# Scaling the memory part of a gated attention on ScalarE instead of VectorE, one head sooner, with another bank order for the last head

## The reference, cut to what matters

```python
q, k, v = x @ Wq.T, x @ Wk.T, x @ Wv.T
qh = q.reshape(b, s, N_QUERY, N_HEAD, D_HEAD)        # 4, 8, 16: 32 heads
scores = jnp.einsum('bsqhd,bthd->bqhst', qh, kh) * scale
probs = jax.nn.softmax(scores, axis=-1)
a_dot = jnp.einsum('bqhst,bthd->bsqhd', probs, vh)
sigma_q = jax.nn.elu(q.reshape(b, s, N_QUERY, D_KV))  # D_KV = 128
a_mem = sigma_q @ memory / (sigma_q @ memory_norm)
w = jax.nn.sigmoid(memory_weight)
out = a_dot * (1.0 - w) + a_mem * w
```

## Time and profile before

| what | us |
|---|---|
| median of 3 runs | 5107.09 |
| lowest and highest | 5098.03, 5112.65 |
| the profiled execution's own time | 5093.37 |
| its span, first to last instruction | 5091.6 |
| PE busy | 4591.6 (90%) |
| DVE busy | 3620.3 (71%) |
| ACT busy | 2409.6 (47%) |
| POOL busy | 716.3 (14%) |

### The profile page before, as it was taken

How to read it: one execution, slowest core, us unless ns; L and a number is a source line. 1 busy time by engine, 2 the same in 40 slices (tenths; PEclk the granted TensorE clock), 3 DMA queues, 4 the chain that set the end, 5 groups by cost and what they waited for, 6 DMA issues and landing times.

```text
span 5091.6 us, 144724 instructions
## 1 busy us (share of the span) xinstructions
PE 4591.6 (90%) x63104; PEld 3229.5 (63%) x63104; DVE 3620.3 (71%) x7890; ACT 2409.6 (47%) x4592; POOL 716.3 (14%) x909
## 2 busy tenths in 40 slices
PE   5799999999999998499999999999999999999998
PEld 4677777777777776346546645655654664665564
DVE  3667766666767666387787678678778767867866
ACT  3234333333333343164564565466456456546645
POOL 0000000000000000112211211221221121122121
PEclk9899999999999998699999999999999999999999
DMA  2222222222222222100000000000000000000000
GB/s 61 48 66 69 65 65 67 61 62 61 62 61 65 64 68 61 64 1 18 1 18 18 18 1 18 18 2 18 18 2 18 18 13 6 18 18 1 18 9 10
DMA packets 352134, 171.76 MB, mean 34 GB/s; under 512 B 300016, under 2 KB 300784, under 8 KB 350736
## 3 DMA queue, kind: packets, MB, share of 16 engines
q1 hardware_dynamic: 342528, 145.20, 10.7%
q10 hardware_dynamic: 8976, 17.30, 1.2%
HBM read 93.74 MB, written 67.63 MB: 32 GB/s over the span
## 4 chain that ended last, share of the span: by engine, by line
PE 43%; DVE 10%; ACT 3%; issue 1%; POOL 1%; DMA 1%; SPq 0%; DVEq 0%; ACTq 0%; POOLq 0%
PE row_psum L1687 9%; PE row_psum L1661 9%; PE row_psum L40 5%; DVE smax L1938 5%; PE row_psum L42 5%; PE row_psum L41 5%; PE row_psum L1675 4%; PE row_psum L1729 1%; ACT xr_hi L1310 1%; PE row_psum L1713 1%; DVE probs L1918 1%; PE row_psum L1451 1%; DVE stats L1772 1%; POOL rstd L1253 1%; PE row_psum L1633 1%
## 5 line engine op out<-in xcount | busy, mean ns | idle before, releaser
L1938 DVE TENSOR_REDUCE smax<-row_psum 128x1 f32<-128x512 f32 x2048 | 1269.3, 681 | 90.9 <-PE row_psum L1661 90.4
L1386 ACT ACTIVATE probs<-row_psum 128x512 f32<-128x512 f32 x2048 | 1096.6, 602 | 378.1 <-PE row_psum L1675 358.5
L1661 PE MATMUL row_psum<-k_stack,q_stack 64*128 64x512 f32 (+1 forms) x2048 | 738.3, 437 | 50.6 <-DVE smax L1938 24.4
L1675 PE MATMUL row_psum<-q_stack,k_stack 64*128 64x512 f32 (+1 forms) x2048 | 761.6, 447 | 17.4 <-DMA q_stack<-shift 4.4
L1661 PEld LDWEIGHTS row_psum<-k_stack,q_stack 64*128 64x128 f32 (+1 forms) x2048 | 350.5, 186 | 504.1 <-DVE smax L1938 374.0
L1687 PE MATMUL row_psum<-probs,v_aug 128*32 128x512 f32 x4096 | 539.5, 604 | 2.3 <-ACT av_sb L1402 0.8
L1675 PEld LDWEIGHTS row_psum<-q_stack,k_stack 64*128 64x128 f32 (+1 forms) x2048 | 340.9, 185 | 211.7 <-ACT probs L1386 152.3
L868 DVE TENSOR_TENSOR lane_t<-lane_t,lane_p 128x30 f32<-128x30 f32 (+14 forms) x960 | 318.3, 332 | 33.0
L40 PE MATMUL span_bank<-x_hi,w_hi 128*128 128x256 f32 x1024 | 303.1, 296 | 32.5 <-DVE x_lo L841 32.5
L865 DVE TENSOR_TENSOR lane_p<-lane_t 128x30 f32<-128x30 f32 (+14 forms) x960 | 315.6, 329 | 23.5
L40 PE MATMUL row_psum<-wf_hi,xr_hi 128*128 128x320 f32 (+1 forms) x1024 | 327.1, 319 | 0.5 <-DVE xr_lo L1806 0.3
(11 more groups left out here) (209 smaller groups left out, 9867.4 us busy)
## 6 DMA issues: line engine op xcount, KB each, us to landing
x_sp<-in_x ACTq DMA_DIRECT2D x33, 512.0 KB, 4.0
tri_dram<-tri SPq DMA_DIRECT2D x256, 64.0 KB, 2.0
lane_t<-tri_dram SPq DMA_DIRECT2D x32, 512.0 KB, 4.7
inv_dram<-lane_t SPq DMA_DIRECT2D x32, 512.0 KB, 2.6
inv_b<-inv_dram SPq DMA_DIRECT2D x256, 64.0 KB, 2.3
x_res<-in_x SPq DMA_DIRECT2D x32, 512.0 KB, 3.9
x<-x_res SPq DMA_DIRECT2D x32, 512.0 KB, 3.7
xs<-x SPq DMA_DIRECT2D x16, 1024.0 KB, 5.6
```

Of the source, the lines that this page charges most:

```text
L1386: act.activation(probs[:, h % PROBS, tt, :], ps[:, m % STACK_BANKS, :], ACT.Exp, scale=float(DH) ** -0.5).then_inc(exp_ready, 1)
L1661: pe.matmul(ps[:, bank, :], q_stack[rows, qt, P * st:P * st + P], k_stack[rows, kv, :], start=True, stop=True).then_inc(max_mm, 1)
L1675: pe.matmul(ps[:, m % STACK_BANKS, :], k_stack[rows, kv, P * tt:P * tt + P], q_stack[rows, qt, :], start=True, stop=True).then_inc(score_m ...
L1938: dve.tensor_reduce(smax[:, g, st:st + 1], ps[:, bank_of("max", NT * g + st), :], AX.X, ALU.max).then_inc(max_ready, 1)
```

## The change

`MEM_LAG` goes from 5 to 4, so the memory steps are at heads 4 to 7 and bank 7 enters the ring at step 8. DVE only takes the reciprocals and weights them; ACT, behind its two exponentials (or q copies) and the shift copy of the step's second half, scales four products of 128 columns by one column each of `mem_rc` and signals `amem_ready`. For the four maxima of head 31 the ring passes bank 7 over.

```diff
-MEM_LAG = 5
+MEM_LAG = 4
...
-                        put("max", NT * g + st)
+                        put("max", NT * g + st, next(n for n in order if g < NH - 1 or n != RING_LAST))
...
+                def memory(t):
+                    act.wait_ge(mem_rc_ready, at(b, NT, t + 1))
+                    for n in range(NQ):
+                        c0 = (DKV + 1) * (n % 2)
+                        last = act.activation(a_mem[:, t, DKV * n:DKV * n + DKV], ps[:, 6 + n // 2, c0:c0 + DKV], ACT.Copy,
+                                              scale=mem_rc[:, t, n:n + 1])
+                    last.then_inc(amem_ready, 1)
...
+                        if j == 1 and 0 <= g - MEM_LAG < NT:
+                            memory(g - MEM_LAG)
...
                     mark(dve.reciprocal(rc, pv[:, :, :, DKV]))
                     dve.wait_ge(dve_own, own[0])
-                    mark(dve.tensor_scalar(rc, rc, mem_w[:, 0:1], None, ALU.mult))
-                    dve.wait_ge(dve_own, own[0])
-                    for c in range(2):
-                        last = dve.tensor_tensor(a_mem[:, t, 2 * DKV * c:2 * DKV * c + 2 * DKV].rearrange("p (n e) -> p n e", n=2),
-                                                 pv[:, c, :, 0:DKV],
-                                                 rc[:, c, :].rearrange("p (n o) -> p n o", o=1).to_broadcast([P, 2, DKV]), ALU.mult)
-                    last.then_inc(amem_ready, 1)
+                    dve.tensor_scalar(rc, rc, mem_w[:, 0:1], None, ALU.mult).then_inc(mem_rc_ready, 1)
```

More of the change, by code:

```diff
@@ L1135, in token_layers @@
         ksel_mm = sem("ksel_mm"); keven_ready = sem("keven_ready"); kodd_ready = sem("kodd_ready"); qsel_mm = sem("qsel_mm"); qstack_ready = sem("qstack_ready")
-        mem_mm = sem("mem_mm"); amem_ready = sem("amem_ready"); amem_added = sem("amem_added")
+        mem_mm = sem("mem_mm"); mem_rc_ready = sem("mem_rc_ready"); amem_ready = sem("amem_ready"); amem_added = sem("amem_added")
         max_mm = sem("max_mm"); max_ready = sem("max_ready"); maxT_mm = sem("maxT_mm"); shift_ready = sem("shift_ready"); shift_in = sem("shift_in")
```

## The result

| | us | against the kernel before, run beside it |
|---|---|---|
| changed kernel, median of 7 runs | 5124.7 (5114.0 to 5131.7) | 1.0056 [1.0037, 1.0074] |
| kernel before, median of 7 runs | 5098.0 (5089.9 to 5112.7) | |
| changed kernel, profiled execution | span 5124.5 | before: 5091.6 |

The change makes the kernel 0.56% slower, 28.5 us by the ratio. The forecast was +13.0 us, or 5120.1. That time is only 4.6 us off, and this is luck in good part: the kernel before now has a median 9 us lower (5098.0 of 7 runs for 5107.1 of 3). Of the difference that came, the forecast had half, and its +13 us, a ratio of 1.0025, lie outside the interval. It had given the case within 0.3% a chance of 0.48 and the case slower by more, which came, 0.39.

The account below looks back on a forecast made before the run. The loop over banks 6 and 7, level with DVE's own work, was taken to bound the memory stretch. Its 27.4 us loss less 14.4 gained at the last head gave +13.0, 5120.1 us against the 5107.1 median; range 5095 to 5140.

Parts of the forecast that it names:

- the loop level with DVE: Heads 5 to 8: loop of reciprocals, scaling, PE's memory matmuls and maxima paces equally with DVE's own work, 0.08 us apart.
- ACT's group: Four scaling copies of 128x128 on ACT per memory step: 1.18 us, bounds 0.83 and 1.48.
- The forecast for the loop: From DVE's max(g,2), head g's tile 2 reduction, through ACT's scaling to PE's memory matmuls: 2.30 us, before 1.88.
- PE's parts: From PE's memory matmuls to DVE's next max(g,2): 1.89 us at head 5, 2.36 at head 6, 1.64 at head 7.
- The part behind the last tile: Head 8: max(8,0) takes bank 7 and waits for the last scaling; PE's part from there to DVE is 0.54 us.
- The start: Memory matmuls of tile 0 now precede q pick 10 on PE, making max(4,2) 0.35 us late.
- The memory stretch: Up to max(8,3), head 8's last reduction: 17.84 us instead of 16.13, so 1.71 us more a batch, 27.4 in all.
- From max(8,3) on, DVE's stream is unbroken in both: After head 8's last reduction DVE runs without breaks before and after the change, with no further cost counted.
- The last head: Head 31: PE's 1.60 us wait for the last maxima goes; 0.85 us gained in 15 batches, 1.6 once, 14.4 in all.
- gives all 1.6: Rival at the last head: the whole 1.6 us wait is gained each batch, total +1.8 us, 5109; chance 0.08.
- only moves: Rival at the last head: the wait moves wholly to the normalised rows' transposes, total +27.4 us, 5134.5; chance 0.08.
- the dearer ACT group: Rival: ACT's scaling group costs over 1.22 us; 1.27 gives +18.4 us (5125.5), 1.48 gives +32.2 (5139); chance 0.31.

Follow-up runs that it names:

- experiment 4: Changed kernel with two ACT copies of 128x256 per group instead of four of 128x128, half the heads using a neighbour's divisor: 5089.0 us, ratio 1.0001 to the kernel before.
- experiment 8: experiment 6 with PE's memory matmuls and DVE's reciprocals moved behind each head's fourth maximum, ACT scaling: 5041.8 us, ratio 0.9934 to the kernel before.
- experiment 9: The order of experiment 8 with the scaling on DVE instead of ACT: 5060.8 us, ratio 0.9968 to the kernel before.
- Experiment 5: Changed kernel with eight extra matmuls on PE ahead of the wait of max(8,0), their results overwritten: 5111.4 us, ratio 1.0042 to the kernel before.
- experiment 6: Changed kernel with bank 7 joining the ring at step 9 instead of 8: 5080.0 us, ratio 1.0011 to the kernel before.
- experiments 7: The kernel of experiment 2 with bank 7 joining the ring at step 9, scaling on DVE: 5091.4 us, ratio 1.0032 to the kernel before.
- experiment 2: Kernel before with memory steps at heads 4 to 7 and the last head's new bank order, scaling still on DVE: 5104.9 us, ratio 1.0020.
- experiment 3: Changed kernel with MEM_LAG 5 again, so ACT scales but memory steps stay at heads 5 to 8: 5128.4 us, ratio 1.0070 to the kernel before.
- experiment 1: Kernel before with only the new bank order for the four maxima of head 31: 5072.5 us, ratio 0.9963.

## Why the prediction was right, and where it fell short

- **The kernel's bound, the loop level with DVE: right.** Experiments 4, 8 and 9 show it from three sides: the shorter group shortens every turn, and with a short loop DVE's own work sets 3.54 us a head, as it did at heads 7 and 8 before.
- **ACT's group, 1.18 us: right,** 1.14 measured. (The 775 ns that the prediction sets beside the Trainium skill's figures, which by two pointer operands give an estimate of 798 ns, are 3% under them and not 2%; nothing hangs on it.) The forecast for the loop, 2.30 us from max(g,2) to PE's matmuls, came out at 2.27 (2393.34 to 2395.61, 2397.51 to 2399.78), and PE's parts 1.89, 2.36, 1.64 at 1.90, 2.37, 1.63. The part behind the last tile, 0.54, is 0.50 with the clock at full speed (2592.93 to 2593.43 in batch 2) and 0.80 in batch 1.
- **The start, 0.35 us late: 0.47.** max(4,2) before began at 2388.46, as the next reduction in a group of ten stands 0.60 behind the last, not 0.618; dividing a group's time by its count took the tail of the last one in. After, it is 2393.34 - 2389.28 = 4.06 us behind the same place instead of 3.59.
- **The memory stretch, +1.71 us a batch: +1.60 in a clean batch** (0.47 + 17.38 against 16.25, up to max(8,3)). Of the forecast idle times, 1.4, 1.8, 1.1 and 1.3, the trace has 1.34, 1.81, 1.06 and 1.23 (1.53 where the clock has fallen).
- **"From max(8,3) on, DVE's stream is unbroken in both": wrong after the change.** Before, 18 reductions run on to 2415.7, and 0.37 us of idle follow; after, three breaks of 0.19, 0.16 and 0.37 us stand there in batch 2. That is 0.35 us a batch more, and the clean period says 0.4 (2.0 less 1.60). It had been read off the trace of before, where nothing was late at this point. What exactly PE lacks there I did not isolate.
- **The last head, -0.85 us a batch: -1.00.** The error is 2 us in all. The rival "gives all 1.6" asked for 9 us more than was there, the rival "only moves" for 17 less.
- **The clean sum** is then 15 x (2.0 - 1.0) + 2.0 - 1.6 = 15.4 us, where 13.0 was forecast. The forecast's own terms were off by 2.4 us, partly against each other. By the medians of the clean periods, 0.95 us a batch in place of 1.04, it is a us or two less.
- **The missing term is the clock.** The forecast named a wait of bank 7 for the last scaling and 1.3 us of idle DVE from it, and stopped there: it priced the wait of DVE and never asked what an idle PE would do to PE. Against the kernel before, the changed one has 15.5 us more in its batches with a fall, and 3.6 us less scatter in the others, so 12 us net, 0.8 a batch. Experiments 5 and 6 take the falls behind the memory part away, by work in the wait and by no wait. With it the sum is 15.4 + 12 = 27 us, where the medians differ by 26.7; the 12 us are what the clean sum leaves over, not a term measured by itself.
- **"Slower" came for a cause that had no chance of its own.** Its 0.39 were the dearer ACT group (0.31) and the lost gain of the last head (0.08). The group was cheaper than forecast and the gain larger, so neither happened.
- **Of the wrong signs named ahead,** none occurred: DVE was not unbroken, the copies were not under 300 ns, and no q copy was so late that PE's wait for it grew (PE's maxima waited 8.4 us in all for L1350 before, and 8.4 after).

## What to carry over

A step moved to a faster or freer engine brings time only if the loop that it stands in gets shorter; add up the loop through every engine, wait by wait, before counting what the old engine is spared. If work has to wait for the step, first put that wait where nothing urgent stands behind it: here this, with bank 7 one head later (by itself +0.11%), turned +0.56% into -0.66%. And price a new wait of TensorE twice, as the wait itself and as the slow matmuls that may follow.

## What the runs showed of the hardware

The granted TensorE clock is touchier than I expected. Behind the memory part it fell from 2.4 to 1.2 GHz in 8 to 16 of 16 batches where the longest wait of PE there was 1.24 us with shorter ones beside it (experiments 7 and 9, 11 each), 1.80 (experiment 2, 11), 1.86 (experiment 4, 8), 2.16 (the change, 14) or 2.19 us (experiment 3, 16). Waits of 0.69, 1.03 and 1.03 us and three small ones, as in experiment 6, were followed by none. But the long wait isn't needed: with waits of up to 0.98 us the clock fell in 1 batch before the change and in 2 in experiment 1, with waits of up to 0.57 us in 2 in experiment 8, and in 2 batches of experiment 3 it fell ahead of the wait of 2.19 us, 1.3 us behind the last of three waits of about 1.03. Experiment 5 has three falls with no such wait near.

Behind the single long waits (experiments 2 to 4 and the change) the fall came between 0.2 us ahead of the wait's end and 2.0 us behind it, and it lasted 3.4 to 10.2 us, even where PE was busy throughout. By the periods of fallen batches against clean ones of the same kernel a fall costs between nothing (experiment 9, batch 7, 3.4 us at half clock) and 2.6 us (experiment 4, batch 1, 10.2 us at half clock: 184.55 against 181.97). Why one batch falls and the next, with the same waits, does not (experiment 4) stays open.
